# A token encoder, a selective-scan block and two gated MLPs: fewer copies of C in DRAM, a share of C's product on GpSimd, five slots for states, squares ahead of decays

## The reference, cut to what matters

```
x: 64 series of 750 samples -> 10 overlapping patches of 128 samples each = 640 tokens, width 512
h  = patches @ W.T + b
u  = layernorm(h)
    h1 = rmsnorm(u) @ in_proj.T  ->  z, xv, B, C, dt_in
    dt = softplus(dt_in @ dt_proj.T + bias)            # 1024 channels
    A  = -exp(A_log);  dA = exp(dt * A)                # 1024 channels x 16 states
    s_t = dA_t * s_(t-1) + (dt*x)_t * B_t              # over a series' 10 tokens
    y_t = sum over the 16 states of C_t * s_t          # C: its own 16 values per group of 16 channels
    y  = (y + D * x) * silu(z);  r = u + y @ out_proj.T
    u2 = r + (silu(n @ gate.T) * (n @ up.T)) @ down.T  # n = rmsnorm(r)
h  = h + u2
h  = h + gated MLP(layernorm(h))
```

## Time and profile before

| | us |
|---|---|
| median of 3 runs | 678.93 (676.79 to 680.03) |
| the profiled execution, its own time | 676.66 |
| its span, first to last instruction | 674.7 |

### The profile page before, as it was taken

The page is one execution under the profiler, slowest core; times in us unless marked ns, Lnnn a source line. Parts: engine busy times, 40 slices in busy tenths (PEclk is TensorE's granted clock), DMA queues, the critical chain, the costliest instruction groups (busy, mean ns, idle before and its releaser), DMA issues.

```text
span 674.7 us, 8618 instructions
## 1 busy us (share of the span) xinstructions
PE 630.5 (93%) x2846; PEld 505.2 (75%) x2846; DVE 425.5 (63%) x660; ACT 329.3 (49%) x646; POOL 428.9 (64%) x244
## 2 busy tenths in 40 slices
PE   4959998799999979999979999999999999999998
PEld 3637675466665657777747777766999998999998
DVE  4087997889987859889887988861322223332132
ACT  4358888458887363323346323321642443543441
POOL 0276786348787999887877988644455464445561
PEclk9979999799999979999989999999999999999999
DMA  8799997599999949989866998634443353144421
GB/s 339 253 358 365 316 312 245 169 280 371 336 375 373 362 176 359 412 334 332 316 247 231 345 326 317 200 124 113 140 153 127 124 157 125 63 128 131 147 67 43
DMA packets 49164, 163.50 MB, mean 242 GB/s; under 512 B 4320, under 2 KB 18528, under 8 KB 48480
## 3 DMA queue, kind: packets, MB, share of 16 engines
q1 hardware_dynamic: 49120, 162.95, 69.6%
HBM read 145.24 MB, written 17.69 MB: 242 GB/s over the span
## 4 chain that ended last, share of the span: by engine, by line
PE 73%; DVE 12%; ACT 4%; POOL 4%; issue 3%; DMA 2%; SPq 0%; DVEq 0%; ACTq 0%; POOLq 0%
PE work L990 53%; PE da L990 15%; DVE da L781 7%; PE work L1000 5%; DVE hs L792 3%; POOL hs L453 2%; ACT L528 1%; DMA bb<-b_rows 1%; ACT da L551 1%; DMA c_rows<-c_rows 1%; DMA sm<-small 1%; POOL acc L479 0%; POOL acc L477 0%; POOL hs L466 0%; DVE a L847 0%
## 5 line engine op out<-in xcount | busy, mean ns | idle before, releaser
L781 DVE TENSOR_TENSOR_SCAN da<-da,hs 128x290 f32<-128x290 f32 (+1 forms) x256 | 198.1, 817 | 35.1 <-POOL hs L453 21.2
L453 POOL TENSOR_TENSOR hs<-dtx,bb 128x1160 f32<-128x1160 f32 (+1 forms) x64 | 171.1, 2674 | 59.6 <-PE work L1000 52.4
L551 ACT ACTIVATE da<-dt,a_neg 128x261 f32<-128x261 f32 (+1 forms) x256 | 118.4, 495 | 144.7 <-DVE hs L792 144.5
L432 POOL TENSOR_TENSOR ws<-wraw,ws 128x1024 fp32r<-128x1024 f32 x40 | 101.5, 2538 | 92.8 <-ACT ws L559 92.8
L990 PE MATMUL work<-sq,wraw 128*128 128x290 f32 x512 | 126.0, 407 | 1.5 <-DVE sq L880 1.1
L990 PE MATMUL work<-hn,win 128*128 128x290 f32 (+1 forms) x336 | 103.6, 457 | 17.4 <-DVE hn L855 8.0
L990 PEld LDWEIGHTS work<-sq,wraw 128*128 128x128 f32 x512 | 96.5, 189 | 30.8 <-issue 1.8
L792 DVE TENSOR_TENSOR hs<-da,cb 128x580 f32<-128x580 f32 (+1 forms) x128 | 105.3, 822 | 10.2 <-DMA cb<-c_rows 3.5
L990 PEld LDWEIGHTS work<-hn,win 128*128 128x128 f32 x336 | 65.7, 200 | 51.3 <-issue 26.1
L559 ACT CAST ws<-wraw 128x1024 fp32r<-128x1024 f32 x48 | 50.3, 1048 | 70.6 <-PE da L990 34.4
L990 PE MATMUL work<-hn,ws 128*128 128x350 f32 x480 | 79.2, 323 | 1.6 <-DVE hn L951 1.6
(11 more groups left out here) (97 smaller groups left out, 630.8 us busy)
## 6 DMA issues: line engine op xcount, KB each, us to landing
wraw<-w_stream SPq DMA_DIRECT2D x104, 512.0 KB, 3.8
bb<-b_rows SPq DMA_DIRECT2D x32, 700.0 KB, 6.7
cb<-c_rows SPq DMA_DIRECT2D x32, 700.0 KB, 5.5
bb<-b_rows SPq DMA_DIRECT2D x32, 580.0 KB, 8.2
cb<-c_rows SPq DMA_DIRECT2D x32, 580.0 KB, 6.2
c_rows<-c_rows SPq DMA_DIRECT2D x8, 875.0 KB, 11.0
c_rows<-c_rows SPq DMA_DIRECT2D x8, 725.0 KB, 6.4
win<-w_in SPq DMA_DIRECT2D x4, 1024.0 KB, 13.1
```

The source lines that it names most:

```text
L432: nc.gpsimd.tensor_tensor(ws[:, k % NW, 1, :], wraw[:, split_loads[k] % NRAW, :], ws[:, k % NW, 0, :].bitcast(F32), ALU.subtract).then_inc ...
L453: nc.gpsimd.tensor_tensor(hs[:, u % NH, 0:NQ * n].rearrange("p (n t) -> p n t", t=n), dtx[:, t % 2, 0:n].unsqueeze(1).to_broadcast([P, NQ, ...
L551: last = nc.scalar.activation(dst, src, ACT.Exp, scale=a_neg[:, j:j + 1])
L781: nc.vector.tensor_tensor_scan(da[:, k % ND, 0:w], da[:, k % ND, 0:w], hs[:, u % NH, p * w:(p + 1) * w], 0.0, ALU.mult, ALU.add).then_inc( ...
```

## The change

- `c_dram` and `b_dram` hold rows in another order, each tile's rows in 32 blocks of 4 rows, 32 rows apart. C is written 2 times over instead of 5, with one DMA each (2 issues per tile, 145 or 175 KB each, for 1 of 725 or 875 KB). B is written 8 times over, 8 issues per half (for 1 with 5 copies). `load_c` reads 32 blocks, each for 4 partitions, which is how `load_b` read already. The channels of a tile are assigned to partitions in another order to suit.
- Prologue: the projection of B's second half moves from before `dtp` and `in_c` of tile 0 to after `in_c` of tile 1, so SP stores it in the slot of unit 1. Each half of B has its own semaphore; the second half is waited for at m = 4.
- In chunk 0 the units with q = 1 (8 of 32) are multiplied by C on GpSimd, in one instruction of 1160 columns; their scans write to `hs` instead of PSUM. GpSimd does this a slot later, behind the next `input_term`.
- `hs` has five slots in chunk 0, four in chunk 1; chunk 1's are larger, so each overlaps two of chunk 0's.
- On ACT, `rms2` and `ln2_var` of chunk 0 are cut into squares (first part of the slot, ahead of the next unit's decays) and inverse root (second part). The table set with Ln is loaded before the root instead of before the squares, and after `rms2`'s slot the set with tanh is loaded at once.

```diff
+HS = 5 * NQ * TS[0]
-NH, NB, ND, NC = 4, 4, 4, 3
+NB, ND, NC = 4, 4, 3
+NH = (5, 4)
+FIRST_SLOT = (0, 2)
-COPIES = (REPL + NQ - 1 + NQ - 1) // NQ
+COPIES, SHARE = 2, 4
+def slot_at(u):
+    c = u // UNITS
+    return (u % UNITS + FIRST_SLOT[c]) % NH[c] * NQ * TS[c]
+def slot_before(u):
+    def ends(v):
+        return slot_at(v) + NQ * TS[v // UNITS]
+    shared = [v for v in range(u) if slot_at(v) < ends(u) and slot_at(u) < ends(v)]
+    return max(shared, default=None)
+def on_pool(u):
+    return u < UNITS and u % QU == 1
 def recurrence(u):
+    if on_pool(u):
+        return [("scan", u, p) for p in range(4)]
...
-    ("in_dt", 0), ("in_b", 0, 0), ("in_b", 0, 1), ("dtp", 0, 0), ("in_c", 0, 0), ("in_x", 0, 0), ("xs", 0, 0)]),
-    (None, [("in_c", 0, 1), ("in_x", 0, 1)])]
+    ("in_dt", 0), ("in_b", 0, 0), ("dtp", 0, 0), ("in_c", 0, 0), ("in_x", 0, 0), ("xs", 0, 0)]),
+    (None, [("in_c", 0, 1), ("in_b", 0, 1), ("in_x", 0, 1)])]
...
+        def multiplied(eng, u):
+            if on_pool(u):
+                eng.wait_ge(c_times_pool, u // QU + 1)
+            else:
+                eng.wait_ge(c_times, products_through(u))
...
             def store_c(c, m):
                 freed(sp, ("in_c", c, m))
-                sp.dma_start(c_dram[c][m].rearrange("(k p) t -> p k t", p=P),
-                             c_rows[:, m % 2, 0:TS[c]].unsqueeze(1).to_broadcast([P, COPIES, TS[c]])).then_inc(
-                                 c_stored[m % 2], 16)
+                dst = c_dram[c].rearrange("(k o m n) t -> k m o n t", k=COPIES, m=KI, n=NQ)
+                for k in range(COPIES):
+                    sp.dma_start(dst[k, m], c_rows[:, m % 2, 0:TS[c]]).then_inc(c_stored[m % 2], 16)
             def load_c(u):
                 if u >= NC:
-                    sp.wait_ge(c_times, products_through(u - NC))
+                    multiplied(sp, u - NC)
...
-                src = c_dram[c][m].rearrange("(o i n) t -> o i (n t)", i=4, n=NQ)[2 * q:2 * q + 2 * REPL]
+                rows = c_dram[c].rearrange("(o m n) t -> m o (n t)", m=KI, n=NQ)[m, 8 * q:8 * q + 32]
+                src = rows.unsqueeze(1).to_broadcast([32, P // 32, w])
...
                     if s[0] == "in_b":
+                        for k in range(COPIES):
+                            for d in range(SHARE):
+                                sp.dma_start(dst[k, d, i], sq[:, 2 + i, 0:TS[c]]).then_inc(b_stored[i], 16)
...
+            def times_c(u):
+                c, w = u // UNITS, NQ * TS[u // UNITS]
+                pool.wait_ge(c_loaded[u % NC], 16 * (u // NC + 1))
+                pool.wait_ge(scan_done, piece(u, NQ - 1) + 1)
+                nc.gpsimd.tensor_tensor(states(u, 0, w), states(u, 0, w), cb[:, u % NC, 0:w], ALU.mult).then_inc(c_times_pool, 1)
...
+                if unit is not None and unit >= 1 and on_pool(unit - 1):
+                    times_c(unit - 1)
...
-                    act.wait_ge(c_times, (k - ND) // 2 + 1)
+                if k >= ND and on_pool(piece_of(k - ND)[0]):
+                    act.wait_ge(scan_done, k - ND + 1)
...
+                    norm = [s for s in steps if s[0] in ("rms2", "ln2_var")]
+                    if norm:
+                        n = steps.index(norm[0])
+                        between = [steps[n - 1]] if steps[n - 1] == SEAM[2] else []
+                        first = steps[:n - len(between)] + [("squares",) + norm[0]]
+                        second = between + [("root",) + norm[0]] + steps[n + 1:]
...
-                    log_tables()
+                    use_tables("exp_and_others" if ("rms2", 0) in steps else "natural_log_exp_and_others")
...
+                dst = states(u, p * w, (p + 1) * w) if on_pool(u) else da[:, k % ND, 0:w]
+                nc.vector.tensor_tensor_scan(dst, da[:, k % ND, 0:w], states(u, p * w, (p + 1) * w), 0.0,
```

More of the change, by code:

```diff
@@ L77, in piece, with piece_of @@
     return PIECE0[c] + u % UNITS * NP[c] + p
+def piece_of(k):
+    u = k // NP[0]
+    return (u, k % NP[0] // 2) if u < UNITS else (UNITS + (k - PIECE0[1]) // NP[1], (k - PIECE0[1]) % NP[1] // 2)
+def on_pool(u):
+    return u < UNITS and u % QU == 1
 def products_through(u):
-    return piece(u, NP[u // UNITS] - 1) // 2 + 1
+    return 2 * len([v for v in range(u + 1) if not on_pool(v)])
+PRODUCTS = products_through(NCH * UNITS - 1)
 def recurrence(u):
+    if on_pool(u):
+        return [("scan", u, p) for p in range(4)]
     return [("scan", u, 0), ("scan", u, 1), ("times_c", u, 0), ("scan", u, 2), ("scan", u, 3), ("times_c", u, 1)]
@@ L260, in build @@
         bb_loaded = [sem(f"bb_loaded{i}") for i in range(NB)]
-        b_stored = sem("b_stored")
+        b_stored = [sem(f"b_stored{i}") for i in range(2)]
         out_stored = sem("out_stored")
@@ L362, in load_b @@
                     sp.wait_ge(dbx_done, u - NB + 1)
[L363 to L366, removed]
+                if q == 0 and m % 4 == 0:
+                    b_in_dram(sp, c, m // 4)
+                rows = b_dram[c].rearrange("(o m n) t -> m o (n t)", m=KI, n=NQ)[m, 8 * q:8 * q + 32]
+                src = rows.unsqueeze(1).to_broadcast([32, P // 32, w])
                 sp.dma_start(bb[:, u % NB, 0:w], src).then_inc(bb_loaded[u % NB], 16)
@@ L446, in input_term @@
                 pool.wait_ge(bb_loaded[u % NB], 16 * (u // NB + 1))
[L447 to L453, removed]
+                v = slot_before(u)
+                if v is not None and v < UNITS:
+                    pool.wait_ge(h_summed, v + 1)
+                elif v is not None:
+                    pool.wait_ge(added, adds_through(v + 1 if v % QU == 0 else v))
+                nc.gpsimd.tensor_tensor(states(u, 0, NQ * n).rearrange("p (n t) -> p n t", t=n),
                                         dtx[:, t % 2, 0:n].unsqueeze(1).to_broadcast([P, NQ, n]),
@@ L596, in step @@
                 kind, c = s[0], s[1]
-                n = TS[c]
+                n = TS[s[2] if kind in ("squares", "root") else c]
                 if kind == "tokc":
@@ L626, in step @@
                     nc.scalar.activation(bank(var), rstd[:, 0:n], ACT.Exp, scale=-0.5).then_inc(rstd_done, 1)
-                elif kind == "rms2":
-                    squares("rms2", c, res_done)
-                    inverse_root(s)
+                elif kind in ("rms2", "ln2_var"):
+                    step(("squares",) + s)
+                    step(("root",) + s)
                     if c == NCH - 1:
[L631 to L636, removed]
+                        hn2_high(c, ("rms2", "ln2_var").index(kind))
+                elif kind == "squares":
+                    squares(*{"rms2": ("rms2", s[2], res_done), "ln2_var": ("ln2", s[2], centered2)}[s[1]])
+                elif kind == "root":
+                    log_tables()
+                    inverse_root(s[1:])
                 elif kind == "in_c":
@@ L787, in times_c @@
                 w = GS[c] * TS[c]
-                here = slice(2 * j * w, 2 * (j + 1) * w)
+                lo, hi = 2 * j * w, 2 * (j + 1) * w
                 if j == 0:
@@ L997, in state_sum @@
                     pe.wait_ge(y_done, m)
-                pe.wait_ge(c_times, products_through(u))
+                multiplied(pe, u)
                 for i in range(NQ):
-                    last = nc.tensor.matmul(work[SUM][:, 0:n], sm[:, S_IDENT:S_IDENT + P], hs[:, u % NH, i * n:(i + 1) * n],
+                    last = nc.tensor.matmul(work[SUM][:, 0:n], sm[:, S_IDENT:S_IDENT + P], states(u, i * n, (i + 1) * n),
                                             start=(q == 0 and i == 0), stop=(q == QU - 1 and i == NQ - 1))
@@ L1125 @@
     part, ng = np.arange(P), P // NS
-    chan = np.concatenate([m * P + NS * (part % ng) + part // ng for m in range(KI)])
+    chan = np.concatenate([m * P + NS * (part // 4 % ng) + 4 * (part // 32) + part % 4 for m in range(KI)])
     c_row = (np.arange(NQ)[:, None, None] * NQ + NS * np.arange(ng)[:, None] + np.arange(NQ)).reshape(P)
-    b_row = (np.arange(NQ)[:, None, None, None] * NQ + NS * (2 * np.arange(KI)[:, None] + np.arange(2)[:, None, None])
-             + np.arange(NQ)).reshape(XB)
-    state = NQ * ((np.arange(NS) // NQ + part[:, None] // ng) % NQ) + np.arange(NS) % NQ
+    b_row = (NS * (2 * np.arange(4)[:, None, None, None] + np.arange(2)) + np.arange(NQ)[:, None, None]
+             + NQ * np.arange(NQ)[:, None]).reshape(P)
+    state = NQ * ((np.arange(NS) // NQ + part[:, None] // 32) % NQ) + np.arange(NS) % NQ
     x = g["x"][:, :, 0]
```

50 lines of the change are left out of this document (27 added, 23 removed).

## The result

| | before | after |
|---|---|---|
| median, same sessions (11 runs each) | 678.32 (676.79 to 680.70) | 681.57 (680.01 to 685.13) |
| the profiled execution, own time / span | 676.66 / 674.7 | 682.28 / 680.2 |

The ratio of after to before is 1.0050, 95% interval [1.0034, 1.0065]: slower by 3.3 us, at the edge of what can be told from no change. The forecast was 3.6 us faster. The profiled execution of before lies 1.7 us under its median and that of after 0.7 us over its own, so distances between the two profiles come out some 2.4 us larger than those between medians.

What follows compares the result with a forecast made beforehand. TensorE was taken as the bound in nearly every stage. Gains of 1.5 + 0.5 + 1.8 - 0.2 = 3.6 us took the profiled 676.66 to 673.1, or 675.3 against the median 678.93; range 669 to 681.5.

Steps and rivals of the forecast that it cites:

- The start: Up to GpSimd's first product: half of B's projection leaves the path; 1.5 us gained, ends 0 and 2.0.
- 40 to 66: The stretch 40 to 66 us: fifth slot and shorter unit 1 cut GpSimd's waits; 0.5 us gained, ends -1.5 and 3.0.
- GpSimd's product: C's product on GpSimd with five slots: 0.4 us for each of two tiles, 1.0 in 103 to 126; 1.8 gained.
- The seam: Where five slots meet four larger: squares 2.6 us sooner, unit 34's input term 2.8 later; net 0.2 us lost.
- `ln2_var`: Chunk 0's second norm: squares already stood ahead of the next decays, decays move into ScalarE's wait for the mean; 0.
- C: Rival, chance 0.13: C arrives late, 1.6 us at each of seven tiles; 686, or 682.5 with only the crowded tiles.
- D: Rival counted within the forecast's 0.45: GpSimd becomes the bound in 66 to 103, giving back two tiles' 0.8 us; 676.
- A: Rival, chance 0.20: TensorE's half-speed matmuls after idle at three places go, 5.9 us besides; 670.
- B: Rival, chance 0.22: seam costs 2.8 us, start's gain is used up on the ramp; 678 to 679.9, no change.

Runs made afterwards that it cites:

- run 4: The kernel before with only the new DRAM rows of B and C and the new channel and prologue order: 681.89 us, ratio 1.0052.
- run 12: The kernel before with only the new layout, B's second half's eight stores spread one per slot over units 4 to 11: 677.80 us, ratio 0.9991.
- run 2: The changed kernel with the eight stores of B's second half issued one per slot in units 4 to 11: 678.86 us, ratio 1.0007.
- run 1: The changed kernel with each half of B stored by two DMAs of 580 KB instead of eight of 145 KB: 680.87 us, ratio 1.0035.
- run 10: The kernel before with only the squares ahead of the decays and the root behind them: 675.46 us, ratio 0.9952.

## Why the prediction was wrong, step by step

- **The start, 1.5 us gained: 0.** The issue time was right (eight at most 4.8 us; 5.13 measured, C issued at 26.51 where 26.3 was worked out). The choice was not: the last of the eight stores goes out at 25.87 and lands 2.87 us later, and B's first load, which waits for it, couldn't be earlier than before (28.76 against 28.54), whatever left TensorE. My own term "from 21.5, to 26.3, against 26.50" gave at most 0.2; I took three quarters of the other end.
- **40 to 66, 0.5 gained: 4.75 lost up to the first gate in the profiles, 3.5 to 4 us in the medians (runs 4 and 12).** This is the step that failed. The prediction named the cause, "SP's eight issues and the 1160 KB in front of unit 3's C", and gave it an end of 1.5 us. It counted eight issues at the start (4.8 us) and didn't count the same eight again here, where C goes out 6.6 us later. The row for the price was there: 8 x 0.60 us from the earlier trace rows. The argument "the total stored by then is 2900 KB both ways" was about sums; the queue asks for order. Runs 2 and 12 show it: the same issues elsewhere bring back 2.9 us by the ratios in the changed kernel, 4.1 with the layout alone. Fewer issues in the same place (run 1) bring back 1.0, which is inside the noise.
- **GpSimd's product, 1.8 gained: about 0, perhaps a loss.** VectorE fell as worked out (16.25 for 16.3), GpSimd's product took 2.65 us where 2.45 was taken. But the tile stayed at 18.95. The prediction had TensorE as the bound and then gave the tile 0.4 us all the same, from 0.259 us for each instruction to 0.250. TensorE's busy time (18.61) has not moved in any of these kernels: the MLP's mean price is not a tile's, whose pairs of matmuls on 32 rows take 0.75 us for two, and the wait of 0.33 us for ScalarE makes up the rest (18.61 + 0.33 = 18.94). The 1.0 us in 103 to 126 is the 1.7 us seen between gates 2 and 3, of which 1.1 goes back behind them.
- **The seam, 0.2 lost: right, and both of its terms.** "2.6 - 2.8" was worked out; measured from gate 6 are 2.65 for the squares and 2.94 for the slots. Because they cancelled, the forecast passed over the most useful thing in it: take the first without the second.
- **`ln2_var`, 0:** 0.7 us gained, between 361 and 460 us (6.39 to 5.70 of distance). The decays of unit 52 now stand ahead of the root, and a stop of TensorE of 0.43 us for `DVEq` at 373.38 of the kernel before is gone; the one after runs its 128 matmuls in a row.
- A rough sum of what was measured, with the loss of the first stretch from medians and the rest from profiles: 0 - 3.8 + 0 - 0.3 + 0.7 = -3.4, against -3.3 measured.
- **Rivals.** C was the right kind, C arriving late, with another mechanism: it was to come from slower reads (landing 6.3 for 4.6 us; measured 5.3 in the MLP's stretch and 7.2 for 8.3 in 40 to 66) at seven tiles, and it came from SP's order at one. Its 1.6 us per tile isn't worked out either: 10.0 - 9.6 is 0.4. D, GpSimd as the bound, appears only with four slots. A's gap before the squares' matmuls closed in part in run 10, to 2.46 us, and not with five slots (5.81). The half-speed matmuls stayed: the 8 behind the gap took 3.88 us at a granted clock of 0.56, against 4.12 at 0.53 before, so of A's 2.1 us 0.2 came back. What run 10 won is the wait itself. B's loss on the ramp came, larger than the start's whole gain; its loss at the seam was given back by the squares.

The Trainium skill's rule against small transfers, weighed in the prediction (DMA: Bandwidth & Descriptors, Rules for kernel authors), agrees in sign with the queue: 5.60 us for eight stores, 1.69 for two with the same bytes; in the time of the kernel no run here tells them apart. The fixed 2 us for each, which the same page gives under Anatomy of one DMA for DMAs that GpSimd issues, did not appear one behind the other, as said; what appeared on SP's queue is 0.64 us for each (5.13/8). Another rule under the first heading is to issue a DMA early and to wait late on its semaphore, to overlap it with compute; it speaks for unit 3's C ahead of the burst. Run 2, which issues that C at 41.29 instead of 46.90 by moving the burst, agrees.

## What to carry to other kernels

When a DMA step is moved, write out the queue at its new place, one line for each issue, with the name of the first load behind it and the time by which its reader wants it: sums of bytes don't show a burst in front of an urgent load. Where two terms of one sum cancel and belong to separable edits, the forecast is not "no change" but "split the edits". And time taken off an engine beside the one that bounds the stage was worth nothing here, though both were over 90% busy: 1.5 us less of VectorE for each tile left every tile at 18.95 us.

## What was not expected of the hardware

- On SP's queue a store of 145 KB from 128 partitions into rows far apart holds the queue for 0.60 to 0.86 us, so eight took 5.13 to 5.66; the single store of 725 KB of C before took 0.36 at 26.50. Issue time did not follow the bytes.
- One store of four copies (580 KB) into the same rows took 6.2 us to land at the median of 20 to 34 us, the old one of five copies (725 KB) 4.6. In 38 to 54 us, among many loads, it was 7.5 against 8.5 for a store of 725 KB of C before: there the new rows show no loss.
- Single executions of one kernel differ by up to 5.7 us (672.17 to 677.83 in run 10), and its profiled one had 30.78 us between gates 2 and 3 at a clock of 0.83, where the kernel before had 29.27 at 0.88. So the profile of the fastest kernel doesn't show its gain in the span (674.8 against 674.7): it has to be read stage by stage. Why the clock falls more in some executions is left open.
